# Attention by pairs of heads in row groups, with token projections kept as three rounded products

## The reference

```python
# block 0
x = x + tanh(g_xattn[0]) * (softmax(q k^T / 4) v Wo + bo)      # q from layernorm(x), k and v from the context
x = x + tanh(g_ffn[0]) * real(ifft(fft(layernorm(x)) w)) + bias # folded into one 256 x 256 matrix, WF
# block 1
x = x + tanh(g_xattn[1]) * (softmax(q k^T + rel_bias) v wo)
x = x + tanh(g_ffn[1]) * moe(layernorm(x))                     # top 2 of 8 experts, relu(x Wup)^2 Wdown
```

## Time and profile before

| | us |
|---|---|
| median of 3 runs (2338.23 to 2343.16) | 2338.26 |
| profiled execution, its own time | 2336.51 |
| its span, first to last instruction | 2334.3 |
| TensorE / VectorE / GpSimd / ScalarE busy | 1909.4 / 1248.1 / 931.8 / 733.1 |
| mean granted clock of TensorE | 0.962 |

### The profile page before, as it was taken

One profiled execution on the slowest core, in us unless ns is written; L12 is line 12 of the kernel. 1 busy time (PEld: TensorE's weight loads), 2 busy tenths in 40 slices (PEclk: granted clock), 3 DMA queues, 4 the chain that ended last, 5 costly groups with the idle time before them and its releaser, 6 DMA issues.

```text
span 2334.3 us, 43845 instructions
## 1 busy us (share of the span) xinstructions
PE 1909.4 (82%) x13810; PEld 1693.3 (73%) x13811; DVE 1248.1 (53%) x3412; ACT 733.1 (31%) x1461; POOL 931.8 (40%) x1286
## 2 busy tenths in 40 slices
PE   2698988988889888898898988987089888888884
PEld 1687877878778788787787877877077776777773
DVE  2356566666665666666656666554544333333331
ACT  2122223232232322323223223222344444444432
POOL 1334445354353543535445354352223333333333
PEclk7799999999999999999999999989599999999997
DMA  4101101011010110101101001010533333333332
GB/s 115 21 13 34 32 12 44 12 33 33 17 38 12 32 35 18 35 14 30 35 18 35 22 23 40 13 32 19 176 66 61 59 59 58 57 56 59 59 50 30
DMA packets 186837, 93.65 MB, mean 40 GB/s; under 512 B 119832, under 2 KB 180248, under 8 KB 186808
## 3 DMA queue, kind: packets, MB, share of 16 engines
q1 hardware_dynamic: 160648, 57.40, 10.3%
q0 software_dynamic: 26160, 35.87, 8.9%
HBM read 43.77 MB, written 44.39 MB: 38 GB/s over the span
## 4 chain that ended last, share of the span: by engine, by line
PE 43%; DMA 18%; issue 13%; POOL 9%; ACT 8%; DVE 7%; SPq 1%; POOLq 0%; DVEq 0%; ACTq 0%
PE scores L1083 23%; DMA out<-y,ids 16%; PE bank L1083 15%; POOL sorted_rows L680 5%; PE bank L1147 2%; ACT routed L790 2%; ACT t_hi L755 2%; POOL rstd L627 2%; DVE t_lo L900 1%; DVE biased L965 1%; ACT q_hi L760 1%; PE bank L1291 1%; POOL kb_hi L645 1%; ACT pr L773 1%; DMA raw<-w_down_t 1%
## 5 line engine op out<-in xcount | busy, mean ns | idle before, releaser
L708 POOL DMA_INDIRECT out<-y,ids x136 | 211.6, 1556 | 458.2 <-ACT y L814 270.6
L627 POOL TENSOR_TENSOR rstd<-var,half_power 128x2 f32<-128x2 f32 x128 | 90.1, 704 | 567.1 <-DVE var L887 566.4
L1083 PE MATMUL scores<-vb,pr 128*128 128x136 f32 x2048 | 285.3, 282 | 19.3 <-ACT pr_rest L776 19.3
L1083 PEld LDWEIGHTS scores<-vb,pr 128*128 128x128 f32 x2048 | 260.4, 192 | 24.9 <-issue 21.3
L1067 DVE SCALAR_TENSOR_TENSOR h<-scores,relu 128x512 f32<-128x512 f32 x136 | 94.0, 691 | 272.7 <-ACT relu L808 272.7
L938 DVE TENSOR_REDUCE mx<-scores 128x8 f32<-128x512 f32 x256 | 169.5, 683 | 117.0 <-PE scores L1083 117.0
L755 ACT ACTIVATE t_hi<-bank 128x512 fp32r<-128x512 f32 x192 | 114.8, 598 | 357.0 <-PE bank L1147 357.0
L1083 PE MATMUL scores<-q_hi,kb_hi 128*128 128x256 f32 (+1 forms) x640 | 198.1, 310 | 34.5 <-ACT neg_mx L765 34.5
L900 DVE TENSOR_TENSOR t_lo<-bank,t_hi 128x512 fp32r<-128x512 f32 x192 | 132.0, 687 | 130.2 <-ACT t_hi L755 126.4
L680 POOL DMA_INDIRECT sorted_rows<-routed,place x128 | 126.5, 988 | 151.6 <-ACT routed L790 120.5
L1083 PE MATMUL scores<-up_hi,xt_hi 128*128 x272 | 120.4, 443 | 79.4 <-DVE xt_lo L1061 78.9
(11 more groups left out here) (219 smaller groups left out, 5460.0 us busy)
## 6 DMA issues: line engine op xcount, KB each, us to landing
xe<-sorted_rows SPq DMA_DIRECT2D x136, 128.5 KB, 2.0
x<-x_rows SPq DMA_DIRECT2D x32, 256.0 KB, 3.0
out<-x_end SPq DMA_DIRECT2D x32, 256.0 KB, 3.1
vb<-v_main SPq DMA_DIRECT2D x128, 32.0 KB
vr<-v_rest SPq DMA_DIRECT2D x256, 3.2 KB
raw<-w_up_t SPq DMA_DIRECT2D x8, 512.0 KB, 4.6
raw<-w_down_t SPq DMA_DIRECT2D x8, 512.0 KB, 4.6
out<-y,ids POOLq DMA_INDIRECT x136, 3.8
```

Of the source, the lines that this page charges most:

```text
L627: pool.tensor_tensor(rstd[u][:], var[u][:], half_power[:], ALU.pow).then_inc(sem(f"rstd_ready{u}"), 1)
L708: pool.indirect_dma_start(out=acc, out_offset=bass.IndirectOffsetOnAxis(ap=ids[j][:], axis=0), in_=y[j][:], in_offset=None, compute_op=ALU ...
L1083: last = pe.matmul(dst, w, m, start=n == 0, stop=n == len(pairs) - 1)
```

## The change

- **Heads by pairs in row groups.** A pair of heads has 32 channels, so its keys and queries lie on 32 partitions. Keys are spread by parity only (`kb`, one of two heads), and a matmul takes the 32 rows of one pair (`rows = slice(2 * DH * j, ...)`) and writes to bank j; four consecutive matmuls take four different row groups and four banks. `by_query` replaces `by_token`: two steps (one per group of 8 heads), each over all four banks of `sc`, each read by one reduction of 4 x 308 columns. `by_key` has all main tiles in one step, `by_key_rest` the 104 late rows.
- **One buffer for scores.** Both `by_query` steps and `by_key` use the four banks of `sc`, and TensorE waits (`clear`, `hold`) until the reader before is done. `turn`, keys share bank A; all row products and queries bank B; `gate`, `places` and the first `sums` bank C; the maximum, the late rows and the second `sums` bank 4 of `sc`.
- **A new order with six slots.** Queries are at the end of the half before.
- **Projections.** `queries`, `output`, `ffn` stay three products of halves. Keys, values and the gate become plain fp32 products, and the halves of the context and of the router's rows go.
- **Setup.** The bias tables get tiles of their own (`tables`, `bias`) and are made while the first two halves run.
- **Experts.** Rows are sorted in tiles of 256 (`NB = 2`), so 144 blocks of 128; one load brings two blocks; GpSimd waits for `added` before every second block only. The zero rows are 18 DMAs.

```diff
@@ half @@
-            do["queries"](*a)
-            fill(1)
-            do["by_token"](*a, 0)
...
+            do["by_query"](u, t, l, 0)
+            fill(1)
+            do["by_query"](u, t, l, 1)
+            fill(2)
+            do["turn_max"](u, t, l)
+            do["by_key"](u, t, l)
+            do["exp"](u, t, l, 0)
+            do["exp"](u, t, l, 1)
+            fill(3)
+            do["by_key_rest"](u, t, l)
+            do["exp"](u, t, l, 2)
+            fill(4)
+            do["sums"](u, t, l, 0)
+            fill(5)
+            do["sums"](u, t, l, 1)
+            fill(6)
@@ slots @@
+            return {1: [("turn", "a0", u, t), ("turn_low", "a0", u, t), ("output", 0, u, t)], 2: [("norm", 1, u, t)],
+                    3: [("turn", "t1", u, t), ("turn_low", "t1", u, t)], 4: [("ffn", u, t), ("norm", 2, u, t)],
+                    5: [("turn", "t2", u, t), ("turn_low", "t2", u, t)], 6: [("queries", u, t, 1), ("queries_low", u, t, 1)]}
...
+            return {1: [("turn", "a1", u, t), ("turn_low", "a1", u, t), ("output", 1, u, t)], 2: [("norm", 3, u, t)], 4: [("turn", "t3", u, t), ("gate", u, t)],
+                    5: [("choose", u, t)]}
...
+            return {1: [("weigh", u, t), ("places", u, t)], 5: [("send", u, t)]}
@@ gpsimd, the scatter of the experts' results @@
-                    pool.wait_ge(sem("added"), k * (DEEP * 16) + j * 16)
+                    if j % NB == 0:
+                        pool.wait_ge(sem("added"), k * (DEEP * 16) + j * 16)
@@ vector @@
+            def by_query(u, t, l, g):
+
+                dve.wait_ge(sem(f"m_done{u}"), num(t, 2 * G, l * G + g + 1))
+                dve.tensor_reduce(mx[u][:, g, :, 0:2 * NC], sc[:, 0:NJ, 0:NC * PK].rearrange("p j (h s) -> p j h s", s=S),
+                                  AX.X, ALU.max).then_inc(sem("scores_read"), 1)
@@ tensor @@
+            def by_query(u, t, l, g):
...
+                clear("scores", t)
+                if l == 1:
+                    for j in range(NJ):
+                        pe.matmul(sc[:, j, 0:NC * PK], ident_b[:], bias_t[:, g, :, j * PK:(j + 1) * PK], start=True, stop=False)
+                for c in range(NC):
+                    for j in range(NJ):
+                        rows = slice(2 * DH * j, 2 * DH * (j + 1))
+                        last = pe.matmul(sc[:, j, c * PK:(c + 1) * PK], q_hi[u][rows, g, c * P:(c + 1) * P], kb_hi[rows, l, g, u],
+                                         start=l == 0 and c == 0, stop=c == NC - 1)
...
+            def by_key(u, t, l):
+
+                pe.wait_ge(sem(f"q_lo_ready{u}"), num(t, 2, l + 1))
+                clear("scores", t)
+                if l == 1:
+                    pe.wait_ge(sem("bias_lo_ready"), 2)
+                    for j in range(NJ):
+                        for b_ in (bias_hi, bias_lo):
+                            pe.matmul(sc[:, j], ident_r[:], b_[:, j].rearrange("p g t -> p (g t)"), start=b_ is bias_hi, stop=False)
+                for g in range(G):
+                    for n in range(3):
+                        for j in range(NJ):
+                            rows = slice(2 * DH * j, 2 * DH * (j + 1))
+                            k_, q_ = passes(kb_hi[rows, l, g, u, 0:P], kb_lo[rows, l, g, u, 0:P], q_hi[u][rows, g], q_lo[u][rows, g])[n]
+                            pe.matmul(sc[:, j, g * T:(g + 1) * T], k_, q_, start=l == 0 and g == 0 and n == 0, stop=False)
+                pe.wait_ge(sem("neg_mx_ready"), so_far("max", t))
+                for g in range(G):
+                    for c in range(NC):
+                        for j in range(NJ):
+                            rows = slice(2 * DH * j, 2 * DH * (j + 1))
+                            last = pe.matmul(sc[:, j, g * T + c * P:g * T + (c + 1) * P], expand[rows, c, 0:P], neg_mx[u][rows, g],
+                                             start=False, stop=g == G - 1 and c == NC - 1)
...
+            def values(u, t):
+
+                pe.wait_ge(sem("ctx_in"), num(t, 32, 32))
+                clear("B", t)
+                product(bankB[0:S], [(ctx[:, k, u], w[:, WV0 - 5:WV0 - 3, k]) for k in range(NK)]).then_inc(sem(f"v_done{u}"), 1)
+                hold("B", "rows_read", "rows")
```

More of the change, by code:

```diff
@@ L287, in wait, with since, so_far @@
                 engine.wait_ge(sem(name), value)
-        def half(do, a, early, slots):
-            def fill(slot):
-                for stage, *args in slots.get(slot, ()):
+        def since(t, per, value):
+            return value if isinstance(t[0], int) else t[0] * per + value
+        made = {}
+        held = {}
+        def so_far(what, t, each=1, less=0):
+            return since(t, each * EACH[what], each * made[what] - less)
+        COUNTED = {"keys": lambda l, t: f"k{l}", "turn": lambda name, u, t: name if name == "t3" else f"t{u}", "queries": lambda u, t, l: f"q{u}", "values": lambda u, t: "rows",
+                   "output": lambda l, u, t: "rows", "ffn": lambda u, t: "rows", "sums": lambda u, t, l, c: f"v{u}", "gate": lambda u, t: "gate",
+                   "places": lambda u, t: "ranks", "turn_max": lambda u, t, l: "max", "by_key_rest": lambda u, t, l: "rest",
+                   "by_query": lambda u, t, l, g: "scores", "by_key": lambda u, t, l: "scores"}
@@ L295, in fill, with half @@
+        STAGES = ("queries", "queries_low", "by_query", "turn_max", "by_key", "by_key_rest", "exp", "sums", "turn", "turn_low", "output", "norm", "ffn", "gate",
+                  "choose", "columns", "weights", "places", "weigh", "send", "stats0", "spread", "keys", "values", "values_out", "loads", "load_x",
+                  "store_x", "tables", "bias")
+        def half(do, u, t, l, slots):
+            def fill(n):
+                for stage, *args in slots.get(n, ()):
                     do[stage](*args)
-            do["queries"](*a)
+            do["by_query"](u, t, l, 0)
@@ L363, in part1_order @@
         def part1_order(do, fori):
-            every = ("queries", "by_token", "join_max", "queries_low", "turn_max", "by_key", "exp", "sums", "turn", "turn_low", "output",
-                     "norm", "ffn", "gate", "choose", "columns", "weights", "places", "stats0", "spread", "weigh", "send", "split_ctx", "keys", "values",
-                     "values_rest", "values_out", "keys_taken", "loads", "load_x", "store_x")
-            do = {name: do.get(name, lambda *args: None) for name in every}
@@ L371, in first_half, with count, counted @@
-            def first_half(t, before, after):
-                half(do, (0, t, 0), True, steps(before, {2: [("values_out", 1, t)]}, spread_steps(0, 1, t), start_steps(1, t), after))
-            def second_half(t, before):
-                half(do, (1, t, 0), True, steps(before, ffn_steps(0, t), spread_steps(1, 0, t)))
+            def count(stage):
+                run_stage = do.get(stage, lambda *args: None)
+                what = COUNTED.get(stage)
+                def counted(*args):
+                    if what is not None:
+                        made[what(*args)] += 1
+                    run_stage(*args)
+                return counted
@@ L377, in third_half, with first_half, second_half @@
+            made.update(dict.fromkeys(EACH, 0))
+            held.clear()
+            do = {stage: count(stage) for stage in STAGES}
+            def first_half(t, *more):
+                half(do, 0, t, 0, steps(*more, {4: [("values", 1, t), ("values_out", 1, t)]}, start_steps(1, t), {3: [("keys", 1, t)], 4: [("spread", 1, 0, t)], 6: [("spread", 1, 1, t)]}))
+            def second_half(t, *more):
+                half(do, 1, t, 0, steps(ffn_steps(0, t), *more))
             def third_half(t, more):
@@ L1223, in sums @@
[L1223 to L1234 removed]
+                hold("B", f"q_lo_ready{u}", f"q{u}")
@@ L1252, in _ @@
-            pe.wait_ge(sem("setup_vec"), 1)
-            pe.wait_ge(sem("setup_act"), 1)
-            pe.wait_ge(sem("w_split"), 3)
+                pe.matmul(bankC[:, 0:NC * E], before_b[:], flat, start=True, stop=True)
+                pe.matmul(bankC[:, NC * E:2 * NC * E], ones_b[:], flat, start=True, stop=True).then_inc(sem(f"ranks_done{u}"), 1)
+                hold("C", "ranks_read", "ranks")
             part1_order({
-                "keys": keys, "keys_taken": keys_taken, "values": values, "values_rest": values_rest, "turn": turn, "output": output, "ffn": ffn,
-                "queries": queries, "by_token": by_token, "turn_max": turn_max, "by_key": by_key, "sums": sums, "gate": gate,
-                "places": places,
+                "keys": keys, "values": values, "turn": turn, "output": output, "ffn": ffn, "queries": queries, "by_query": by_query,
@@ L1259, in _ @@
+                "turn_max": turn_max, "by_key": by_key, "by_key_rest": by_key_rest, "sums": sums, "gate": gate, "places": places,
             }, pe.Fori)
```

814 lines of the change are left out of this document (368 added, 446 removed).

## The result

The changed kernel takes 2523.8 us (median; 2518.3 to 2525.3), the kernel before, run beside it, 2339.0: a ratio of 1.078, 95% interval 1.076 to 1.080. The forecast was 2392, its range 2300 to 2640. The direction and the range held; the size, +55 us, was measured as +185.

What follows compares the result with a forecast made beforehand. The prediction took TensorE to bound the loop and each scatter's wait for the one before to bound the experts. Its sum was 2336.5 - 39 + 3.9 + 151 + 0.6 + 19 + 11 - 91 = 2392 us, range 2300 to 2640.

Steps and rivals of the forecast that it cites:

- Loop, +151: Loop over pairs: waits around the single score buffer lengthen each pair by 10.05 us, 15 times, +151 us.
- rival 3: Loop: TensorE's clock falls behind the new waits, 2 us lost a half, +128, 2520 us; chance 0.10.
- Setup, -39: Setup: with the bias off the path, the first by_query starts at 48 us, saving 39 (bounds 30 and 45).
- First two halves, +3.9: First two halves, ahead of the loop: the same working of waits as in the loop adds 3.9 us.
- Row groups concurrent: Score matmuls: four 32-row matmuls of different row groups cost as much as one, 0.12 us.
- Rival 1: Score matmuls: row groups load one after the other, +214 us, 2606 us (2530 to 2660); chance 0.27.
- Switches of the tiling, 0.3 us a half: TensorE's switches between whole array and row groups: two on a half's path, 0.3 us a half, 19 in all.
- VectorE's queue between the reductions: Each half: the add and statistics precede the second reduction, so TensorE stands at turn_max from 5.1 to 8.8 us.
- Rival 2: Loop: fewer waits than counted, pair under 102.6 us, so faster: 2272 us (2200 to 2330); chance 0.20.
- Experts, -91: Experts' stage: scatters wait every second block, so TensorE sets the pace at 3.7 us a block, saving 91 us.
- Zero rows, +11: Ahead of the experts' weight loading: nine more zero-row DMAs at 1.26 us each, +11 us.
- Rival 4: Experts' stage: scatters by pairs bring nothing, 2392 + 91 + 37 = 2520 us; chance 0.05.

Runs made afterwards that it cites:

- e5_fill_all: Changed kernel with idle matmuls added before the output projection, the maximum's turn, ffn, the gate and places, more than in e1_fill: 2456.8 us, ratio 1.047.
- e10_bias_in: e14's kernel with the late rows' scores ahead of the turn of ffn's input and the bias tables' roundings inside the second half: 2267.3 us, ratio 0.968.
- e13_double: Changed kernel with VectorE doing the second reduction of every half twice, once into an unread tile: 2606.1 and 2624.1 us, ratios 1.113 and 1.120.
- e4_order: Changed kernel with the second part of the query-side scores ahead of the output projection and its addition: 2375.1 us, ratio 1.014.
- e6_keys_first: e4_order with VectorE doing the keys' low part ahead of the next batch element's statistics and norm, first half of a pair: 2275.9 us, ratio 0.972.
- e2: Changed kernel with every expert scatter waiting for the one before it again, blocks still in pairs: 2634.0 us, ratio 1.125.
- e3: Kernel before with only the changed experts' part (blocks in pairs, scatter waiting every second block, nine more zero-row DMAs): 2264.7 us, ratio 0.967.
- e14: e6_keys_first with ScalarE's four scalings and the places behind the attention rows' turn, rerun on the chip of e15 and e16: 2253.5 us, ratio 0.962.
- e15: e14's kernel with the bias tables' roundings inside the second half, on the same chip as e14: 2248.0 us, ratio 0.960.
- e11: Same kernel as e15 (e14's with the bias tables' roundings inside the second half), on another chip: 2276.7 us, ratio 0.971.
- e16: e3 repeated on the chip of e14 and e15: 2263.7 us, ratio 0.966.
- e1_fill: Changed kernel with idle matmuls added, 14 before the output projection and 16 during the wait for the maximum's reduction: 2475.3 us, ratio 1.056.
- e7_keys_fill: e6_keys_first with idle matmuls added in the remaining waits: 2335.6 us, ratio 0.996.

## Why the prediction was right in direction and wrong in size

- **Loop, +151 with +18 for the switches; measured +267: the step that failed.** The sum was made wholly at the full clock. The two waits of each half stood in it by name and not far from their size, and rival 3 had the mechanism ("now there are waits of 2.8 and 3.7 us in each half") and about its price (+128). I gave it 0.10 as an alternative. It was no alternative: it follows from the forecast's own waits. The loop missed by 98: e5_fill_all puts the low clock at 120 (8 us a pair), and at the full clock the forecast of the loop was 22 too high (1618.9 / 15 = 107.9 us a pair, against 106.5). Rival 3's 2520 is the time that was measured, but that the totals meet is in part luck: the start of the third half added 26 us that it hadn't, and the 22 go against them. Its working is right in what is lost, 2 us a half; but it had 4 us of each half at 1.2 GHz, and by the granted clock of 0.83 it was 9.7 of 28.6, part of it idle.
  The Trainium skill (TensorE: Matmul & The Clock Gate, "HAM oscillation — how this bites in real kernels") tells of a kernel whose matmuls begin cold after every wait. This trace agrees in part: 0.83 in the loop and 0.21 us between starts behind the waits of 3.73 and 3.22 us, but also some way behind a wait of 1.64, and not behind the wait of 1.94 us at 350.73.
- **Setup, -39; measured -28.** `by_query` began at 59.0 and not at 48. In the profile rstd stands behind eight spread operations in GpSimd's queue, then the value products stand ahead of `by_query` at the low clock:

```profile
46.54 0.72 POOL L606 TENSOR_TENSOR rstd<-var,half_power 128x2 f32<-128x2 f32 x1
47.29 0.73 DVE L867 TENSOR_SCALAR xn<-x,mv,rstd 128x256 f32<-128x256 f32 x2 [3.97 <-POOL rstd L606]
...
55.48 3.61 PE L1035 MATMUL bank<-w,ctx 128*77 128x512 f32 x4 [1.93 <-DVE q_lo L891]
...
59.02 0.46 PE L1148 MATMUL scores<-kb_hi,q_hi 32*128 32x154 f32 x8
```

  The roundings took the 6 us that I had (to 37.6); what I had put at 10 took 21. I had added durations and left out the order of the queues.
- **First two halves, +3.9; measured +19.5** (66.0 instead of 46.5). Of this 4.5 to 5.7 us are the roundings of the bias tables, which I had called hidden (e10_bias_in: the third half 4.5 us earlier). The window's clock of 0.77 speaks for the low clock as the rest; that was only read.
- **Row groups concurrent: right.** Four loads and four matmuls in 0.12 us. Rival 1 is dead, and with it the doubt whether loads of different groups overlap (the prediction calls it the second rival; it is the first). The Trainium skill has that (TensorE: Matmul & The Clock Gate, "Packing small matmuls — row/col tiling"), which I had overlooked. The work after the change, by the prediction's own terms, is 65.9 us a pair and not 65.5; the 2392 doesn't use it.
- **Switches of the tiling, 0.3 us a half: about right.** I had no row for it. Measured are 0.19 at one entry at the full clock, by the two distances above, so 0.38 for the two entries on the path.
- **Reduction 1.46: measured 1.44. VectorE's queue between the reductions: right.** e13_double shows it by itself (+92 expected, +88 to +91 measured); e4_order's -148 holds the t_lo wait as well.
- **Rival 2, fewer waits and so faster than before:** its threshold of 102.6 us a pair is not reached in this order. In another order it is: e6_keys_first, 98.9 a pair, is faster than the kernel before.
- **Experts, -91; measured -87.6. Zero rows, +11; measured +10.9. Both right.** e2 and e3 confirm the mechanism from both sides. Rival 4 is dead.
- **Chances.** With the clock inside the sum the forecast would have been 2392 + 128 = 2520, right to 2 us by the luck named above.

A version that beats both kernels: e14 and e15, 0.960 to 0.962 of the kernel before. The old attention with the experts in pairs (0.966) is nearly there, and on the chip of e11 the new attention (0.971) came out behind it, though the old one wasn't run on that chip. What the change gains, then, it gains in the experts (-88); the rest of it, setup and row groups in their best order, is worth at best 0.6% more (e15 against e16). No run takes the row groups without the single buffer for scores, so what each is worth alone stays open.

## What to carry to other kernels

Where a change takes work from TensorE and adds waits, the waits have a second price: the granted clock. Put it into the sum, not among the rivals, as soon as waits like these (1.6 to 3.7 us each, several in every half) recur in the loop. Filling them with added matmuls is no remedy: it brought 67 us of some 120 once and cost 60 the other time, while orders that removed waits brought 148 and 99. With a single buffer between two engines, what decides is the order in the consumer's queue: put what releases the buffer ahead of what nobody waits for yet; here that one move, made in two lists, was worth 148 us. After each such move read again which wait is last, since it may only change its name.

## What the runs showed of the hardware that I had not expected

- Work ran at the low clock behind 2.41 us of idle time too (e5_fill_all: then 0.25 us between starts), and in the changed kernel behind 1.64 (0.21 us), not only behind 3.73.
- One kernel took 2248 us on one chip and 2277 on another, with the kernel before at 2342 and 2344: in the slower one ScalarE's q_hi came 0.3 to 2.5 us later ahead of two of the four halves.
- Executions of some of these kernels spread by 1.1% and follow the granted clock (e1_fill: 2461 at 0.927 to 2488 at 0.917; e7_keys_fill: 2323 at 0.944 to 2347 at 0.933); those of the kernel before by 0.4% at most.
- In the three kernels with 800 to 893 matmuls a pair the turn of the loop held 2.4 to 4.2 us of idle time called issue (e5_fill_all and e7_keys_fill in all 14 turns, e1_fill in 8).
